# Attention, an MLP and an expert layer on one core: the MLP's work beside attention in 256-row items, with one more block there

## The reference

```
x = layernorm(x + attn(x));   x = layernorm(x + ffn(x))

attn(x):  q, k, v = heads(ln(x) @ w_in.T + b_in)      # 16 heads of 16
          rows t % 8 == 0 attend to all 2048 keys, every other row to itself alone
          x = x + softmax(q k / 4) v @ w_out.T + b_out
          x = x + gelu(ln(x) @ w1.T + b1) @ w2.T + b2  # exact gelu, 1024 wide

ffn(x):   e = argmax(x @ gate_W.T + gate_b)            # one of 8 experts
          h = relu(x @ wi.T + wi_b + (x @ A[e].T) @ B[e].T)
          out = h @ wo.T + wo_b                        # 1024 wide
```

## Time and profile before

| what | value |
|---|---|
| three runs | 1439.64, 1443.39, 1442.14 us; median 1442.14 |
| the profiled execution: span from first to last instruction | 1437.3 us (its own time outside the span is not given; the median of the runs is 4.8 us above the span) |
| instructions | 26412, of these 10103 matmuls |
| TensorE busy | 1386.3 us, 96% of the span |
| VectorE, ScalarE, GpSimd busy | 59%, 51%, 45% |
| DMA | 130.51 MB, 91 GB/s on the mean |
| projections b = 0 to 3 (from the first MLP item to attention's) | 111.1, 169.5, 170.0, 170.3 us |
| attentions b = 0 to 3 | 151.4, 173.5, 173.5, 151.3 us |
| tail | 117.2 us |

### The profile page before, as it was taken

One profiled execution on the slowest core, in us unless ns is written; L12 is line 12 of the kernel. 1 busy time (PEld: TensorE's weight loads), 2 busy tenths in 40 slices (PEclk: granted clock), 3 DMA queues, 4 the chain that ended last, 5 costly groups with the idle time before them and its releaser, 6 DMA issues.

```text
span 1437.3 us, 26412 instructions
## 1 busy us (share of the span) xinstructions
PE 1386.3 (96%) x10103; PEld 1066.3 (74%) x10103; DVE 854.4 (59%) x1823; ACT 734.6 (51%) x1103; POOL 647.8 (45%) x533
## 2 busy tenths in 40 slices
PE   6799999999999999999999999999999999999997
PEld 5688665678888766668888866667888876556996
DVE  6748576636656666555647576763675657762332
ACT  3444555553544555564444555555444455655442
POOL 3554321328754414145865432333776442132755
PEclk9899999999999999999999999999999999999999
DMA  7565223215561132212682213220556212310100
GB/s 246 161 181 107 57 45 67 55 38 192 190 164 47 50 68 51 56 45 84 210 214 62 74 38 75 57 53 20 189 189 158 74 45 44 80 26 23 52 16 30
DMA packets 91394, 130.51 MB, mean 91 GB/s; under 512 B 8314, under 2 KB 68180, under 8 KB 88148
## 3 DMA queue, kind: packets, MB, share of 16 engines
q1 hardware_dynamic: 91268, 128.82, 32.9%
HBM read 68.08 MB, written 60.57 MB: 90 GB/s over the span
## 4 chain that ended last, share of the span: by engine, by line
PE 79%; DVE 10%; POOL 4%; issue 2%; ACT 2%; DMA 0%; SPq 0%; POOLq 0%; DVEq 0%; ACTq 0%
PE ps L1567 19%; PE ps L1568 16%; PE ps L1569 16%; PE ps L1756 8%; PE ps L1745 7%; PE ps L1730 4%; DVE mx L1442 3%; PE ps L1803 2%; PE ps L1791 2%; PE ps L1825 2%; DVE stats L1316 2%; POOL rows L1042 1%; ACT prob L1172 1%; PE ps L1688 1%; PE ps L1762 1%
## 5 line engine op out<-in xcount | busy, mean ns | idle before, releaser
L1442 DVE TENSOR_REDUCE mx<-ps 128x2 f32<-128x1024 f32 x256 | 311.1, 1223 | 179.0 <-PE ps L1730 176.9
L1172 ACT ACTIVATE prob<-ps 128x1024 f32<-128x1024 f32 x256 | 262.6, 1026 | 180.4 <-PE ps L1745 180.2
L1057 POOL TENSOR_TENSOR hid1l<-gel,hid1h 128x512 fp32r<-128x512 f32 x85 | 111.2, 1309 | 202.2 <-ACT hid1h L1214 202.1
L1057 POOL TENSOR_TENSOR hid2l<-gel,hid2h 128x512 fp32r<-128x512 f32 x85 | 111.1, 1307 | 197.6 <-ACT hid2h L1214 197.5
L1057 POOL TENSOR_TENSOR hid0l<-gel,hid0h 128x512 fp32r<-128x512 f32 x86 | 112.4, 1307 | 191.6 <-ACT hid0h L1214 191.5
L1206 ACT ACTIVATE gel<-ps,cols 128x512 f32<-128x512 f32 x128 | 88.2, 689 | 180.7 <-PE ps L1569 169.5
L1745 PEld LDWEIGHTS ps<-qslot,kslot 50*128 50x128 f32 x1024 | 76.2, 184 | 91.0 <-issue 65.8
L1208 ACT ACTIVATE gel<-ps 128x512 f32<-128x512 f32 x128 | 76.6, 598 | 120.9 <-PE ps L1825 119.7
L1756 PE MATMUL ps<-prob,vals 128*32 128x256 f32 x2048 | 137.5, 385 | 0.2
L1745 PE MATMUL ps<-qslot,kslot 50*128 50x256 f32 x1024 | 128.9, 330 | 4.2 <-ACT prob L1172 4.1
L1730 PE MATMUL ps<-kslot,qslot 48*128 48x512 f32 x512 | 105.8, 424 | 4.8 <-DVE mx L1442 4.4
(11 more groups left out here) (245 smaller groups left out, 3943.9 us busy)
## 6 DMA issues: line engine op xcount, KB each, us to landing
k_d<-kst SPq DMA_DIRECT2D x192, 128.0 KB
kslot<-k_d SPq DMA_DIRECT2D x64, 384.0 KB
xin<-in_L_attn_x SPq DMA_DIRECT2D x32, 256.0 KB, 4.3
rows<-xs_d SPq DMA_DIRECT2D x16, 512.0 KB, 6.3
y_d<-rows SPq DMA_DIRECT2D x15, 512.0 KB, 3.1
rows<-y_d SPq DMA_DIRECT2D x15, 512.0 KB, 4.5
out<-rows SPq DMA_DIRECT2D x15, 512.0 KB, 3.2
xs_d<-xin SPq DMA_DIRECT2D x28, 256.0 KB, 2.7
```

The costliest lines, as they stand in the source:

```text
L1057: nc.gpsimd.tensor_tensor(hid[i % RING][1][:], gel[i % 2][:], hid[i % RING][0][:], ALU.subtract).then_inc(lo_done, 1)
L1172: nc.scalar.activation(prob[(n - 1) % 2][:].rearrange("p e i q -> p (e i q)"), ps[:, 0:2, :].rearrange("p a n -> p (a n)"), ACT.Exp).then_ ...
L1442: nc.vector.tensor_reduce(best[:, :, j % NQ], ps[:, at:at + 2, :], AX.X, ALU.max).then_inc(maxr_done, 1)
```

## The change

The block M(b,3) moves from the projection to attention, as its first block; attention's order is then M(b,3), F(b-1,0), F(b,1), F(b,2), with 24 items for b = 0 and 3 and 32 for b = 1 and 2. All blocks beside attention are `NARROW`: an item is 256 rows and 256 of the middle's columns. Each `up` half now gives one 128-column tile of the middle for 256 rows, and Gelu is called once for each tile, since each has its own bias column. The down-product of a narrow block contracts each half of the array's rows by itself into its own bank; VectorE adds both banks, after four items for the first 256 rows and after eight for the others. In the list of steps an item is: up 0, (a step), up 1, a turn if one is due, Gelu and `hid`, a step, down 0, down 1, a step; the step after up 0 is there in the first item only where there are 32, and in 17 of 24 elsewhere. The turns of this stage move from bank `UP` to the maxima's banks. The activation `gl` is now a step of its own. The projection's maxima are brought closer together to fit into eight items less.

```diff
-    _beside = ([("F", _b - 1, 3)] if _b else []) + [("M", _b, 1)] + ([("M", _b - 1, 0)] if _b else []) + [("M", _b, 2), ("M", _b, 3)]
+    _beside = ([("F", _b - 1, 3)] if _b else []) + [("M", _b, 1)] + ([("M", _b - 1, 0)] if _b else []) + [("M", _b, 2)]
...
-    _beside = [("F", _b, 1)] + ([("F", _b - 1, 0)] if _b else []) + ([("F", _b, 2)] if _b + 1 < B else [])
+    _beside = [("M", _b, 3)] + ([("F", _b - 1, 0)] if _b else []) + [("F", _b, 1)] + ([("F", _b, 2)] if _b + 1 < B else [])
...
+NARROW = [what == "attention" for what, _ in PHASE]
...
-            twos = (10, 12, 14, 16, 17, 19)
+            twos = (9, 10, 11, 12, 13, 14)
...
-            twos = (16, 17, 24, 25, 32, 33)
+            twos = (16, 17, 20, 21, 26, 27)
...
+        more = STEPS_B - 1 - 2 * (n - 1)
+        for j in range(n):
+            i = FT * blocks[0] + j
...
+            put(("up", i, 0))
+            if (j + 1) * more // (n - 1) > j * more // (n - 1) if more > 1 else j == 0:
+                step()
+            put(("up", i, 1))
+            pending.append(i)
+            if j == n - 1:
+                weighted(STEPS_B - 2)
+                weighted(STEPS_B - 1)
+            hook = {0: [("tn", ready, 0)], 1: [("tn", ready, 1), ("xw", ready)], 3: [("ga", ready)], 7: [("pi", ready)]}.get(f, [])
+            for one in hook:
+                put(one)
+            if alone:
+                for one in alone.pop(0):
+                    put(one)
...
+            put(("gl", i))
+            put(("ev", i))
...
+            if j < n - 1:
+                step()
+            down(0)
+            down(1)
+            if j < n - 1:
+                step()
...
-        _banks = [UP if _beside else OUT]
+        _banks = [(MX if _w in ("mt", "ot") else MX + 1) if _beside else OUT]
...
+                    elif NARROW[i // FT]:
+
+                        for g in range(2):
+                            c = B1C + 2 * (f % HF) + g
+                            last = nc.scalar.activation(gel[i % 2][:, AW * g:AW * g + AW], ps[:, UP, AW * g:AW * g + AW], ACT.Gelu,
+                                                        bias=cols[:, c:c + 1])
...
+                    part = flat(y[:, 2 * h:2 * h + 2, :])
+                    if NARROW[k]:
+
+                        dve.wait_ge(down_done, FT * k + HF * (h + 1))
+                        for e in range(2):
+                            if e:
+                                dve.wait_ge(sum_done, SUM_AT[(k, h)] - 1)
+                            nc.vector.tensor_tensor(part, part, ps[:, DOWN + e, :], ALU.add).then_inc(sum_done, 1)
...
+                        rest = slice(AW * (f // HF), AW * (f // HF) + AW)
+                        tile = 2 * (f % HF) + k
+                        for m in range(KT):
+                            last = three(ps[:, UP, AW * k:AW * k + AW], [t[:, m, P * tile:P * tile + P] for t in wup[w]],
+                                         [t[:, m, rest] for t in turned[blk % 2]], k == 0 and m == 0, w == "M" and m == KT - 1)
...
+                        tile = 2 * (f % HF) + h
+                        high, low = wdn[BLOCKS[blk][0]]
+                        for j in range(2):
+                            at = AW * h + P * j
+                            for r, (one, w) in enumerate(((0, high), (0, low), (1, high))):
+                                for e in range(2):
+                                    half = slice(HALF * e, HALF * e + HALF)
+                                    last = mm(ps[:, DOWN + e, D * j:D * j + D], hid[i % RING][one][half, at:at + P], w[half, tile, :],
+                                              start=f % HF == 0 and h == 0 and j == 0 and r == 0,
+                                              stop=f % HF == HF - 1 and h == 1 and r == 2, skip_group_check=True)
```

More of the change, by code:

```diff
@@ L94, in down, with close @@
             pending.pop(0)
[L95 to L104, removed]
+            close(i)
+    def close(i):
+        if NARROW[i // FT]:
+            if i % HF == HF - 1:
+                put(("sum", i // FT, i % FT // HF))
+        elif i % FT == FT - 1:
+            for h in range(2):
+                put(("sum", i // FT, h))
     def piece(b, q, part):
@@ L284, in turns @@
                 alone.insert(0, [("mt", b, p + 1), ("mtd", b, p + 1)])
[L286 to L294, removed]
         def moves(s):
@@ L305, in moves, with step @@
                         put(("ldx", b + 1, CHUNKS[q]))
-                for at, one in ((53, ("pa", b + 1, CHUNKS[0])), (55, ("pb", b + 1, CHUNKS[0])), (58, ("pt", b + 1, CHUNKS[0])),
-                                (60, ("pa", b + 1, CHUNKS[1]))):
+                for at, one in ((53, ("pa", b + 1, CHUNKS[0])), (55, ("pb", b + 1, CHUNKS[0])), (60, ("pa", b + 1, CHUNKS[1]))):
                     if s == at:
                         put(one)
-        def step(s):
+                if s == 58:
+                    alone.append([("pt", b + 1, CHUNKS[0])])
+        taken = [1]
+        def step():
+            s = taken[0]
+            if s >= STEPS_B:
+                return
+            taken[0] += 1
             if s % 2 == 0:
@@ L315, in step @@
                 weighted(s - 1)
-            scores(s)
+            put(("sc", b, s // KK, s % KK))
             maxima(s)
@@ L322, in step @@
                 put(late.pop(0))
-        s, hook = 1, []
-        places = [(0, 2, 4, 7)] * 2 if len(blocks) == 2 else [(0, 2, 3, 7), (0, 1, 3, 7), (1, 2, 4, 7)]
-        for quarter in range(4 * n):
-            ahead = min(2, quarter // 2) if len(blocks) == 2 else 0
-            while s < STEPS_B and s * 4 * n <= (quarter + ahead) * STEPS_B:
-                step(s)
-                s += 1
-            i, part = FT * blocks[0] + quarter // 4, quarter % 4
+        more = STEPS_B - 1 - 2 * (n - 1)
@@ L366, in attention @@
-        assert s == STEPS_B and not alone and not late
-        weighted(STEPS_B - 2)
-        weighted(STEPS_B - 1)
+            put(("up", i, 0))
[7 more added lines that the diff above has]
+            hook = {0: [("tn", ready, 0)], 1: [("tn", ready, 1), ("xw", ready)], 3: [("ga", ready)], 7: [("pi", ready)]}.get(f, [])
@@ new lines, in attention @@
+            for one in hook:
+                put(one)
+            if alone:
+                for one in alone.pop(0):
+                    put(one)
+                    if one[0] == "ot":
+                        late.append(("os", *one[1:]))
+            put(("gl", i))
+            put(("ev", i))
+            after(k - 1, f, 4)
+            rows_in(k, f, 6)
+            for part in {4: (0, 1), 5: (2, 3)}.get(f, ()):
+                put(("pick", ready, part))
+            if j < n - 1:
+                step()
@@ L370, in tail @@
+            down(0)
+            down(1)
+            if j < n - 1:
+                step()
+            while late:
+                put(late.pop(0))
+        assert taken[0] == STEPS_B and not alone and not late, (taken, alone, late)
     def tail(b):
@@ L468 @@
         FINAL[_s[1:]] = AT * (len(FINAL) + 1)
+SUM_AT = {}
+for _s in STEPS:
+    if _s[0] == "sum":
+        SUM_AT[_s[1:]] = max(SUM_AT.values(), default=0) + (2 if NARROW[_s[1]] else 1)
 IN, MX, OUT, UP, DOWN, KQ = 3, 2, 4, 5, 6, 2
```

86 lines of the change are left out of this document (38 added, 48 removed).

## The result

The changed kernel takes **1542.4 us** (median of 4 runs, 1541.0 to 1545.5), the kernel before, run beside it, 1440.9. The ratio is 1.071, 95% interval 1.069 to 1.073: slower, as forecast, but by 101 us where some 45 were predicted, and outside the range of 1455 to 1525. The profiled execution has a span of 1543.6 us, 106.3 above the one before.

The account below looks back on a forecast made before the run. TensorE was taken as the bound, with ScalarE's table loads deciding in M items. Terms -38 + 4 - 15 + 88 + 6 = +45 on the 1437.3 us span gave 1482, about 1488 us as median; range 1455 to 1525.

Parts of the forecast that it names:

- the plain M item: M item in attention without copies of turns: ScalarE's chain from scores B to the next scores B, 6.8 us.
- rival C: A table change also empties ScalarE for as long again as the load: +83 us, 1571 us; chance 0.03.
- the price of a change of kind: On TensorE in attention, one change between kinds of matmul costs about 0.2 us.
- the shortened projections: Projections after losing a block: VectorE late by some 3 us at b = 0, 1 each elsewhere; +6 us together.
- rival B: Row halves of the down-product do not run side by side: +114 us, 1600 us; chance 0.03.
- Rival A: Table loads fall into ScalarE's idle time in attention, so the 88 us vanish: -43, 1399 us; chance 0.10.
- list of signs: What would show the forecast right: 64 more table loads, attentions of about 190 and 208 us, projections shorter by 23 to 25.
- Waits in F items: In attention's F items, scores would hardly wait for Exp and maxima would just fit VectorE's reduction: -15 us.
- Rival D: VectorE bounds the F items, a third of 80 waiting 1 us: +27, 1515 us; chance 0.12.
- Loads, + 88: Attention's M items: two table loads each on ScalarE's chain, +20 us per 32-item attention, +24 per 24-item one; +88 together.
- Order: Steps grouped around down halves in attention: 157 changes of kind become 97 or about 123; -38 us together.
- A load costed at nothing: F block row loads on SP in attention: rows wanted an item or more later, as before; no cost.

Follow-up runs that it names:

- experiment 2: Kernel before with Gelu in place of Relu in the first F block of every attention, adding 64 table loads in the old order: 1474.5 us, ratio 1.023.
- the run with Relu: Changed kernel with Relu in place of Gelu in the M blocks beside attention, so 64 table loads less: 1450.3 us, ratio 1.006.
- experiment 8: Exp, maxima's reduction, or both halved: on the run with Relu 1445.0, 1414.2, 1409.8 us; on the kernel before, reduction alone 1427.5, both 1421.0.
- experiments 5 and 6: 5: changed kernel, third step between down halves 1566.0 us; sums moved too 1555.8; Gelu before copies too 1496.0. 6: kernel before, new order in 24-item attentions, 1458.3.
- a fill: Changed kernel with 18 unread 256-column matmuls more per M item beside attention, ahead of scores waiting for Exp: 1549.0 us, ratio 1.076.
- experiment 7: Kernel before, its blocks, step order and turns' bank kept, with 256-row up-products and row-half down-products beside attention: 1454.9 us, ratio 1.010.

## Why the prediction was right or wrong

**Right.** The direction and its cause, 64 table loads on the chain from scores to scores; the plain M item (6.97 for 6.8); the price of a load, 1.28 us, so rival C is out; the price of a change of kind; the shortened projections; the row halves, which ran side by side (six pairs in 0.70 us: rival B is out). Rival A is out in this order; in the old one more than half of the loads' 82 us (64 x 1.28) was hidden (experiment 2). The Trainium skill, "ScalarE: Activation LUTs", What ACT_TABLE_LOAD costs, gives about 2.66 us with a drain; in the timeline above a load begins at 542.80, where the Exp before it ends (541.76 + 1.03), and the Exp behind the next load begins 1.29 us after that load's start (547.10 after 545.81), so the measurement decides against it here. The fit of the 32-item F blocks (142 us) is partly luck: by the prediction's own terms these attentions come to some 204 us (173.5 + 25.8 + 1 - 12 - 4 + 20), not to the 208 of its list of signs.

**"Waits in F items", - 15: the step that failed.** The sums above put the waits of the four attentions at 30 us before and 62 without any table load: + 33 for - 15, the largest miss. Its half on Exp was right: ahead of the scores the weight loads wait 6.2 us for Exp in the run with Relu, for 21.9. Its half on the maxima was not. The prediction gave the reduction 1.7 of 1.88 us and the turns "hidden, with nothing to spare", and priced both at nothing. It did that by the rhythm of 32 items, where the waits indeed grew by only 2.5 us an attention. In the first and last attention, where 17 of 24 items hold a third step, they went from 10 to 27 and 21, and in the last maxima and turns stand 10 us on the same two banks, for VectorE (rows in experiment 8). Halving the reduction takes 27 us off the four attentions with Relu and 13 off those before. Moving the third step did not help (experiments 5 and 6); how much the order costs here and how much the turns' move to these banks stays open. Rival D (+ 27 on top of the forecast, 0.12) named this engine and queue.

**Loads, + 88: measured 98 (92 by the medians).** The term was right but for one thing. With 32 items it was 20 and, with the clock held by a fill, measured at most 19.7; the fall to 1.2 GHz added at least 5.9 in each of those two attentions. The prediction read 1.00 from the stretches before and did not ask what the clock would do where TensorE waits.

**"Order", - 38: measured - 33.** The price of 0.2 us held, in the old order and in the new. The changes as run are 103 and 130, a few more than the 97 and 123 of the forecast.

**A load costed at nothing.** "The F rows are wanted an item or more later, as before" failed in the first attention. In the run with Relu TensorE waits 3.5 us there for the row load, and the clock falls behind it; both are within the 27 us of waits above and are probably most of the 7 us that the first attention takes over the last.

```profile
139.91 0.63 PE L1802 MATMUL ps<-ident,rows 128*128 128x128 f32 x4 [3.49 <-DMA rows<-y_d]
```

```profile
143.00:148.20 5.20, 5.20 (x34) 3.53 (x34) 1.10 (x1) 0.52 (x2) 0.92 (x1) 0.54 0.02 3
```

Together the attentions missed by 61 us (852.6 measured; 752.9 + 39 forecast): the waits 48, the loads 10, the order 5, and the narrow forms 2 the other way.

No form of the change beats the kernel before: the best that keeps all its work, experiment 7, is 1.0% slower. The control with half of the maxima's reduction is 0.9% faster than the kernel before (0.988 to 0.994). A maximum only shifts the exponents, and the shift cancels when the weighted sums are divided; so what that kernel leaves out does not change the softmax as long as no Exp overflows, though the expectation above calls the output another one.

## What to carry to other kernels

Before work whose activation needs another table is put beside Exp, follow one buffer round its loop (scores, Exp, load, Gelu, copy, load, Exp): it is the loop's length that the item takes, and copies queued ahead of Gelu lengthen it. An average of free ScalarE time says nothing about it. A price per change of kind is worth only as much as the count, and the count has to take in the changes that the new form itself brings. A wait that is taken from one bank has to be looked for at the next, in the stage with the most steps to an item and not in the one with the fewest.

## What the runs showed of the hardware that had not been expected

The granted clock fell in the middle of the kernel, in a block where TensorE was busy for 59.6 of 75.3 us (0.84 on average, spells at 0.50), while the same block with the copies moved, busy for 49.9 of 59.7, kept 1.00; and a block with more work was shorter (69.4 for 75.3 us) at a clock of 1.00.
